# Sinkhorn rounds in which TensorE makes the fourth group's column products one step earlier

## The reference

```python
K = jnp.exp(-M / MU)
K = K / jnp.maximum(K.sum(axis=(-2, -1), keepdims=True), EPS)
def step(carry, _):
    u, u_prev, v = carry
    diff = jnp.sqrt(jnp.sum((u - u_prev) ** 2, axis=-1))
    active = jnp.max(diff) > TOL
    v_new = c_ / jnp.maximum(jnp.einsum('bnm,bnk->bmk', K, u), EPS)
    u_new = r_ / jnp.maximum(jnp.einsum('bnm,bmk->bnk', K, v_new), EPS)
    ...
(u, _, v), _ = jax.lax.scan(step, (u0, u_prev0, v0), None, length=ITERS + 1)
P = u * K * jnp.swapaxes(v, -2, -1)
```

## Time and profile before

| | us |
|---|---|
| median of 3 runs | 514.15 (514.02 to 514.8) |
| span of the profiled execution | 510.8 |
| a pair of rounds in the loop (spread(3) at 102.55 to spread(3) at 110.82) | 8.27 |
| TensorE busy, 60 to 140 us | 80.00 of 80 |
| VectorE busy, 60 to 140 us | 64.91 of 80 |

### The profile page before, as it was taken

The page is one execution under the profiler, slowest core; times in us unless marked ns, Lnnn a source line. Parts: engine busy times, 40 slices in busy tenths (PEclk is TensorE's granted clock), DMA queues, the critical chain, the costliest instruction groups (busy, mean ns, idle before and its releaser), DMA issues. The chain is left out here.

```text
span 510.8 us, 24000 instructions
## 1 busy us (share of the span) xinstructions
PE 473.7 (93%) x9062; PEld 391.8 (77%) x9062; DVE 353.8 (69%) x1264; ACT 324.2 (63%) x809; POOL 241.7 (47%) x580
## 2 busy tenths in 40 slices
PE   3899999999999999999999998789999989999992
PEld 3689999999986635666666677678888878999991
DVE  5778888888878685767657655568888887645440
ACT  4655555555546864656666567578777778977770
POOL 3644444444445001055443545724677756776552
PEclk9899999999999999999999999999999999999996
DMA  9262000000000066143223000710111116365210
GB/s 249 89 205 86 0 0 0 0 0 0 0 1 1 2 137 151 51 84 84 82 60 112 3 0 2 277 56 4 36 58 47 48 48 187 125 165 151 62 35 10
DMA packets 24221, 34.60 MB, mean 68 GB/s; under 512 B 3632, under 2 KB 17973, under 8 KB 23768
## 3 DMA queue, kind: packets, MB, share of 16 engines
q1 hardware_dynamic: 21376, 27.23, 19.3%
q0 software_dynamic: 2784, 6.56, 3.6%
HBM read 25.98 MB, written 8.26 MB: 67 GB/s over the span
## 5 line engine op out<-in xcount | busy, mean ns | idle before, releaser
L223 ACT ACTIVATE den_v<-ps_g,floor 128x128 f32<-128x128 f32 x124 | 45.3, 367 | 43.8 <-PE ps_g L254 39.6
L268 PE MATMUL ps_g<-buf_b,v_pad 128*32 128x128 f32 x1984 | 67.2, 277 | 0.2 <-issue 0.2
L254 PE MATMUL ps_g<-buf_a,u_pad 128*32 128x128 f32 x1984 | 66.3, 274 | 0.1
L254 PEld LDWEIGHTS ps_g<-buf_a,u_pad 128*32 128x32 f32 x1984 | 53.2, 111 | 0.4 <-DVE u_pad L340 0.3
L268 PEld LDWEIGHTS ps_g<-buf_b,v_pad 128*32 128x32 f32 x1984 | 51.1, 111 | 1.0 <-issue 0.4
L1406 POOL DMA_INDIRECT out<-buf_d,token_i x39 | 38.8, 996 | 23.3 <-DVE buf_c L1909 16.6
L748 PE MATMUL ps_h<-buf_c,up 128*128 128x512 f32 x96 | 49.1, 607 | 0.6 <-DVE buf_c L1027 0.4
L362 DVE RECIPROCAL v_pad<-ps_g 128x32 f32<-128x32 f32 x124 | 38.7, 333 | 14.6 <-PE ps_g L260 12.3
L205 POOL TENSOR_SCALAR held_u<-inv_u 128x8 f32<-128x8 f32 x124 | 24.5, 197 | 39.4 <-DVE inv_u L371 38.7
L1394 POOL DMA_INDIRECT sorted_x<-rows,slot_i x32 | 32.4, 1011 | 20.3 <-DVE slot_i L1850 13.1
L1618 PE MATMUL ps_ss<-xT,buf_d 128*128 128x128 f32 x312 | 41.4, 276 | 0.5 <-ACT xT L1744 0.2
(11 more groups left out here) (370 smaller groups left out, 1238.7 us busy)
## 6 DMA issues: line engine op xcount, KB each, us to landing
cw_b<-cw_d SPq DMA_DIRECT2D x16, 512.0 KB, 7.9
buf_c<-sorted_x SPq DMA_DIRECT2D x39, 136.0 KB, 2.4
buf_b<-in_x_t SPq DMA_DIRECT2D x4, 512.0 KB, 6.2
buf_d<-in_x_nt SPq DMA_DIRECT2D x1, 2048.0 KB, 9.6
x<-in_w SPq DMA_DIRECT2D x1, 2048.0 KB, 8.9
buf_b<-in_w SPq DMA_DIRECT2D x1, 2048.0 KB, 13.2
buf_a<-in_x SPq DMA_DIRECT2D x3, 512.0 KB, 5.5
sorted_x<-nobody SPq DMA_DIRECT2D x1, 1088.0 KB, 12.0
```

Of the source, the lines that this page charges most:

```text
L223: fn(den_v[:, h, :], ps_v[h], ACT.Relu, bias=floor[:]).then_inc(v_den, 1)
L254: last = mm(ps_v[h][32 * j:32 * j + 32, :], u_pad[:, h, j, 32 * i:32 * i + 32], K[:, t * D:(t + 1) * D], start=i == 0, stop=i == TI - 1)
L268: last = mm(ps_u[h][32 * c:32 * c + 32, :], v_pad[:, h, c, 32 * i:32 * i + 32], KT[:, b * N:(b + BG) * N], start=i == 0, stop=i == TI - 1)
```

## The change

In `one_round` on TensorE the wait for `u_ready[3]` and the column products of group 3 move up by one place, from behind turn(1) to the place between turn(0) and turn(1). The other engines' programs stay as they are, and so does every instruction.

```diff
@@ -282,10 +282,10 @@
                     to_columns(2)
                     pe.wait_ge(v_den, i + 1)
                     turn(0)
+                    pe.wait_ge(u_ready[3], i + 1)
+                    to_columns(3)
                     pe.wait_ge(v_den, i + 2)
                     turn(1)
-                    pe.wait_ge(u_ready[3], i + 1)
-                    to_columns(3)
                     pe.wait_ge(v_den, i + 3)
                     turn(2)
                     pe.wait_ge(v_ready, i + 1)
```

## The result

The changed kernel takes 511.03 us (median of six runs, 510.51 to 511.44), the kernel before 513.43 (six runs, 512.06 to 514.8). The ratio is 0.9949, with a 95% interval of 0.9932 to 0.9966: 2.6 us faster by that ratio (2.4 between the two medians), where 1.7 had been forecast. Part of that is the base, since the median of three runs from which the forecast was counted, 514.15, was on the high side.

The account below looks back on a forecast made before the run. VectorE's chain spread(3), invert(0), turn_back(0), spread(3) was taken as the bound, 8.27 us a pair. A gain of 0.11 a pair over 15 pairs gives 1.7; 510.8 − 1.7 = 509.1, plus 3.35 gives 512.4 us, range 511.9 to 514.6.

Parts of the forecast that it names:

- The view of what bounds the kernel: Sinkhorn rounds: VectorE's chain spread(3), invert(0), turn_back(0), spread(3) sets 4.13 us without and 4.14 with a loop branch ahead.
- The moved block: TensorE: column products 3 start 0.24 us behind spread(3) instead of 0.39; turn(3) can load 0.12 us earlier.
- What the gain meets in B: Round behind VectorE's loop branch: turn(3) gains only 0.08 us, making the next round's turn(0) and invert(0) 0.08 earlier.
- the cover of the stream: TensorE from turn(3) to the next turn(0): block 0's load waits 0.02 us, costed at nothing; other end 0.06.
- the prediction's own signs of being wrong: In the round without loop branch: turn_back(0) later than 1.62 us behind spread(3), or turn(0) unmoved; or a longer first round.
- The price: VectorE: invert(1) moves from 0.77 to 1.04 us behind spread(3), delaying invert(2) and turn_back(0); covered in both rounds.
- The first round: VectorE's group multiply by c starts later, but seems to end with GpSimd's: cost 0, other end 1.06 us once.
- The slower one: VectorE's invert(1), invert(2), turn_back(0) each wait for the one ahead's end: 515.2 us; 0.14, including the first round's price.
- The absorbed case: TensorE blocks 0 to 2 each pay 0.02 us behind late weight loads: 513.25 us; 0.30 together with the late block.
- the late block: TensorE sees spread(3) too late, so column products 3 delay turn(1): 513.25 us; 0.30 together with the absorbed case.
- All that follows the rounds: Later stages start from VectorE's last spread(3) and move with it, keeping the rounds' 1.7 us.
- the 3.35 us all around the span: Difference between the runs' median 514.15 and the profiled span 510.8 us, taken to lie around the span and left unchanged.

Follow-up runs that it names:

- the two VectorE edits: turn_back(3) moved ahead of spread(2), and the two waits of invert swapped; both added to the changed kernel: 506.63 us, ratio 0.9876 to the kernel before.

## Why the prediction was wrong, step by step

**The view of what bounds the kernel failed.** Its sentence was "B's 2.47 is that order alone", of VectorE from turn_back(0) to spread(3). It was not. turn_back(1) waited for rows(1) in B too, 0.07 of the 0.13 behind inverse(0). turn_back(2) then waited 0.04 for rows(2): in B it followed turn_back(1) by 0.47 (108.96, 109.43), and follows it by 0.43 in the changed kernel (107.03, 107.46). Together these are the 0.11, and the piece in B is 2.36 without them. The rows shown could have told it: A and B took 4.13 and 4.14, although invert(0) comes 0.05 later in B. Two rounds that are equally long in spite of different delays share a bound in which the delay has no part. Here that was turn(3) to turn(3), 4.13 us apart. I had read a chain from VectorE's rows and filled its pieces with what preceded them, without asking whether each piece had a slack.

**The moved block** was right: s + 0.25 against s + 0.24, and turn(3) at s + 1.38 in A against s + 1.37. In B it came at s + 1.43, against s + 1.42.

**What the gain meets in B, and the cover of the stream,** failed with the view. A's turn(0) is not earlier against spread(3): 100.83 − 100.75 = 0.08, before 0.06. That was one of the prediction's own signs of being wrong. Both moved together, because spread(3) of B itself is earlier by 0.10. So the 0.07 that A's turn_back(0) was to gain is not there (s + 1.63, forecast s + 1.55, before s + 1.62), and the pieces that did shrink are the last ones, 0.08 in A (forecast 0.04) and 0.11 in B (forecast 0). 0.18 a pair instead of 0.11, and 15 pairs give 2.7 us instead of 1.7. That the forecast had the right direction and a gain of this order is in part luck: of its 0.11 the 0.07 that went over A's turn(0) did not come, and other waits gave some 0.14 in its place.

**The price** was right in its instructions: invert(1) comes at s + 1.06 and invert(2) at s + 1.33 (forecast 1.04 and 1.29 to 1.31). That it was covered in A has another reason than the forecast gave: turn_back(0) did not come earlier, and follows invert(2) by 0.30, more than VectorE's queue alone asks, which was 0.21 with the swapped waits.

**The first round** was right. VectorE's multiply starts at 19.41 instead of 18.95, takes 1.56 instead of 2.05 and ends at 20.97 instead of 21.00. GpSimd's own multiply runs to 19.89, and VectorE's ends 1.08 behind it, as in the kernel before. The round's spread(3) starts at 23.61 instead of 23.50. The timeline of the changed kernel has:

```profile
15.07 4.82 POOL L193 TENSOR_TENSOR buf_b<-buf_b,c_t 128x1024 f32<-128x1024 f32 x2 [8.45 <-DVE c_t L350]
19.41 1.56 DVE L357 TENSOR_TENSOR buf_b<-buf_b,c_t 128x1024 f32<-128x1024 f32 x1
```

**The rivals.** The slower one fell: invert(1) at 101.81 lasts 0.36 and invert(2) starts at 102.08, 0.27 behind it. With the swapped waits turn_back(0) starts at 103.04, while the reciprocal ahead of it ends at 103.12. So neither is held for the whole length of the one ahead. The absorbed case and the late block did not happen either: the pair gained 0.18, and the block started at s + 0.25. What happened is a case that was not listed: the wait that the change takes out from in front of column products 3 was part of the bound of both rounds, so both became shorter.

**All that follows the rounds** was to move with them. The two profiled spans differ by 1.5 us only (510.8 and 509.3), though the rounds differ by 2.7. The later stages vary by as much between executions: with turn_back(3) early under the kernel before, whose rounds are as long as before, the profiled span was 512.8 against 510.8. The timed ratios, 0.9949 and 0.9944, have room for the whole 2.7. Which later stage varies was not studied. Nor were the 3.35 us all around the span, as the prediction had it: the changed kernel's profiled execution took 511.04 us with a span of 509.3, 1.7 more, and so it is with every other run. By that the profiled execution of the kernel before took some 512.5 us, and the rest of the 3.35 lies within the spread of its six runs (512.06 to 514.8).

## What to carry to other kernels

When several engines hand work round in a ring, write down every closed loop of waits and add each up; the longest sets the period, as the 4.13 us from turn(3) to turn(3) did in the kernel before, and a chain that is read off one engine's rows shows only that this engine keeps time with it. Rounds that take equally long although one has a known extra delay are a sign that the bound lies elsewhere. And an edit that gains nothing today can be worth its full amount when another loop has been cut: of the two VectorE edits here one was worth nothing under the kernel before and the other nothing clear under the changed kernel, and both with the move took the kernel to 0.988 of its time.

## What the runs showed of the hardware

The profile has two rows for each 32-bit matmul of these kernels. The extra matmul ahead of rows(1) is issued once in each of the 30 rounds of the loop, and the view of its line counts 60:

```profile
L274 PE MATMUL ps_x<-buf_a,ident x60: 272/274/276, 25.4 to 149.2; 128*32 128x128 f32 x60
```

The 8 matmuls of a group's column products are 16 rows, and in the page of the kernel before L254 has 1984 in all, which is 16 for each of 4 groups in 31 rounds.

The order in which the two waits of invert are written was worth 0.09 us in round A. In the changed kernel, with the wait for the turn first, invert(0) starts 0.19 behind the end of turn(0) (101.07 to 101.26). Between the two VectorE's sequencer has an operation of 0.04 us, which the view of L361 shows at 101.2:

```profile
L361 DVEq ALU_OP  x1: 40/40/40, 101.2 to 101.2; - x1
```

The trace has its start at 101.17, 0.10 behind the end of turn(0), and in its operands the wait for the semaphore that the last matmul of turn(0) raises (`$S[136]>=` and `$S[136]++`). With the wait for the turn last, the operation carries the other wait (`$S[130]>=`) and the reciprocal has `$S[136]>=`. There the view of L361 shows the operation at 101.6:

```profile
L361 DVEq ALU_OP  x1: 40/40/40, 101.6 to 101.6; - x1
```

turn(0) ends behind it, and invert(0) starts 0.10 behind that end (101.82 to 101.92). Under the changed kernel alone the order was worth 0.02 a pair (8.10 to 8.08) and nothing clear in the time; with turn_back(3) early, where theory 2 has the loop over invert(0) as the longest, it was worth 0.19 a pair (8.02 to 7.83).

A single profiled execution can hold a pause of its own. In the one with turn_back(3) early under the changed kernel, TensorE idled 1.1 us once, near 30 us, with nothing that the profile shows to wait for, as the list of waits from 20 to 45 us has it:

```profile
PEld ps_g L268 <- issue: 1.1, 1, 1.1
```

In the kernel before the longest such pause in that stretch was 0.4 us, and in the changed kernel TensorE has none there. What caused it was not studied. So a single profiled execution can misstate a gain of 1 us, and the length of a pair in the steady part of the loop is the safer measure.
